# Fifty more unread TensorE products per image, in the filter's overhang and at the two ends of an image

## The chip, the core and the metric

The kernel runs on one core of a Trainium2 chip. The metric is the device time of one launch in microseconds (us), as the median of several runs. The core has five engines with their own instruction streams: TensorE (PE, matrix products; weight loads are shown as PEld), VectorE (DVE), ScalarE (ACT), GpSimd (POOL) and SyncE (SP, which issues the DMAs). They wait for one another by semaphores.

## The reference

The input is x, 16 images of 64 channels and 128 x 128 pixels. Two layers follow one another.

```python
# layer 0
q_in = jnp.quantile(x.reshape(B, C, -1), 0.5, axis=-1)      # a median per image and channel
x = x + relu(-q_in)[:, :, None, None]
y = upfirdn2d(x, lpf, up=2, padding=6, gain=4)              # 7 taps, along rows and columns
y = jnp.maximum(y, 0.0)
y = upfirdn2d(y, lpf, down=2)
# layer 1
spec = rfft2(x); mag = abs(spec)
gate = sigmoid(w2 @ gelu(w1 @ mag))
xf = x + irfft2(spec * gate)
q = xf @ q_w + q_b                                          # 16384 queries, 4 heads of 16
k, v = kv_path(8x8 convolution of xf), kv_path(16x16 convolution of xf)   # 256 + 64 keys
out = (softmax(q k / 4) v) @ proj_w + proj_b + x
```

## The kernel before

One loop runs over the 16 images, with a block for each engine in it. Each iteration does all of one image and, beside it, the median of the image after it. At its end every engine drains and meets the others at a barrier (L1416), SyncE clears the semaphores (L1422), a second barrier follows (L1423), and each engine jumps back to the start of the loop (L1415).

The stages of an image, as TensorE's program (`tensor`, from L392) has them:

1. The filter: 37 rounds n = 0 to 36 (P + 5, with P = 32 pairs of channels). In a round TensorE filters pair n along one direction (L463), pair n - 1 along the other (L473), takes pair n - 2 down again (L484), transposes pair n - 3 (L503) and takes two pairs that end with n - 4 down in the other direction (L494). Between these ScalarE (L1057, L1064) and VectorE (L834, L848, L841) copy the results out of PSUM. In the rounds 32 to 36, the overhang, no new pair enters and the last ones run out of the pipeline. `mid_up`, `mid_across` and `mid_down` (L432 to L450) compute a middle strip of the image every eighth round.
2. The forward transform: 17 rounds with L521 and L536 to L539; VectorE copies with L869 and L873.
3. Gate, inverse transform, convolutions, keys and values.
4. Attention over 32 groups of 512 queries, in 34 steps of ten parts; the last step of all ends with L763, L770 and VectorE's L1009.

The median search is a bisection in 26 steps. In a step VectorE (L304) and ScalarE (L247) each count values in three portions, TensorE adds the counts of two partitions (L203, L204), VectorE compares (L311 to L316), and the next step begins. It is written as generators (`pe_median`, `dve_median`, `act_median`, `pool_median`), which every engine's program advances at fixed places by `slot(n)`. So the order of the work on each engine is written out by hand. In a round of the filter the first `slot` stands behind L473 and, in the overhang, a second one at the round's end.

Unread products: `busy(bank, n)` issues n products of a constant with the identity, 128 x 128 by 128 x 512 in bfloat16, into a PSUM bank whose content nobody needs then. Nothing reads them and they signal nothing (L402). The kernel before has them at the start of an image (2), around the gate, between the small steps of the keys and values, in the first two groups of attention, and at the end of an image (2, 3 and 5 in the last step).

Of the kernel before, what the change touches and what calls it, by code (L numbers as in the profile page):

```python
# [29 lines left out]
P = C // 2  # L30
# [28 lines left out]
def program(nc, xa, xb, lev, msel, xh, small, sr1w, sr2w, out, nb=B):  # L59
    ctx = ExitStack()  # L60
    with ctx:
# [21 lines left out]
        def c(name, rows=128):  # L83
            o, w = SMALL[name]
            return cst[0:rows, o:o + w]
# [306 lines left out]
        def tensor(e):  # L392
# [3 lines left out]
            def slot(n):  # L396
                for _ in range(n):
                    next(med, None)

            def busy(bank, n):  # L400
                for _ in range(n):
                    e.matmul(ps[:, bank, :], lhsT=identb[:, :], rhs=cst[:, 0:256].bitcast(BF16), start=True, stop=True)  # L402

            busy(6, 2)

            def rest_up(b):
                e.wait_ge(xr, b + 1)
# [45 lines left out]
            for n in range(P + 5):  # L453
                if n < P and n % 8 < 3:
                    (rest_up, rest_across, rest_down)[n % 8](n // 8)
                if n < P:
                    if n:
                        e.wait_ge(t1, n)
                    for i in range(2):
                        x = XH[n // 4][:, 2 * (n % 4) + i, :]  # L460
                        for j in range(2):
                            r = slice(64 * j, 64 * j + 64)
                            op = e.matmul(ps[:, j, 133 * i:133 * i + 133], lhsT=x[r, :], rhs=ut[r, 133 * j:133 * j + 133],  # L463
                                          start=True, stop=True)
                    op.then_inc(up_ps, 1)
                m = n - 1
                if 0 <= m < P:
                    e.wait_ge(t1, m + 1)
                    if m:
                        e.wait_ge(yr, m)  # L470
                    for j in range(2):
                        r = slice(64 * j, 64 * j + 64)
                        op = e.matmul(ps[:, 2 + j, :].rearrange("p (c h n) -> p c h n", c=2, h=2),  # L473
                                      lhsT=ut[r, 133 * j:133 * j + 128],
                                      rhs=T1[m % 2][r].rearrange("p h c n -> p c h n")[:, :, :, 0:128], start=True, stop=True)
                    op.then_inc(yw_ps, 1)
                slot(1 if n > 1 else 0)
                m = n - 2
                if 0 <= m < P:
                    e.wait_ge(yr, m + 1)  # L480
                    if m:
                        e.wait_ge(vt, m)
                    for j in range(2):
                        op = e.matmul(ps[64 * j:64 * j + 64, 4, :], lhsT=c(f"d{j}"), rhs=Y[m % 2][:, j, :],  # L484
                                      start=True, stop=True)
                    op.then_inc(dn_ps, 1)
                m = n - 4
                if 0 <= m < P and m % 2:
                    gq = m // 2
                    e.wait_ge(vr, m + 1)  # L490
                    if gq:
                        e.wait_ge(zz, gq)
                    for j in range(2):
                        op = e.matmul(ps[64 * j:64 * j + 64, 6, :], lhsT=c(f"d{j}"), rhs=V[gq % 2][:, j, :, :],  # L494
                                      start=True, stop=True)
                    op.then_inc(z_ps, 1)
                m = n - 3
                if 0 <= m < P:
                    e.wait_ge(vt, m + 1)
                    if m:  # L500
                        e.wait_ge(vv, m)
                    for i in range(4):
                        op = e.transpose(ps[:, 5, 128 * i:128 * i + 128], VT[m % 2][:, 128 * i:128 * i + 128], c("ident"))  # L503
                    op.then_inc(tr_ps, 1)
                if n >= 8 and n % 8 < 3:
                    (mid_up, mid_across, mid_down)[n % 8](n // 8 - 1)
                slot(1 if n >= P or n % 4 == 0 and n > 8 else 0)

            for n in range(17):
                slot(1)  # L510
# [117 lines left out]
            def stage(g, j, bk):  # L628
                v0 = 16 * g + 4 * j
                bank = b7 if bk == 7 else b6  # L630
                e.wait_ge(*bank[0])
                if g == 0:
                    e.wait_ge(xfa, 8)
                e.matmul(ps[:, bk, :], lhsT=c("qw"), rhs=XFT[:, v0:v0 + 4, :], start=True, stop=True).then_inc(q_ps, 1)  # L634
                bank[0] = (qr, 4 * g + j + 1)
# [144 lines left out]
            for t in range(NT + 2):  # L780
                u, s4, ahead = t // 4, t % 4, t + AHEAD
                live, prev, done2 = t < NT, 0 <= t - 1 < NT, t >= 2
                for w in range(10):
# [17 lines left out]
                        denominators(t - 1)  # L801
                    if (t, w) in STAGES:
                        stage(*STAGES[t, w])
            busy(0, 5)

# [607 lines left out]
        with nc.Fori(0, nb, hint_back_edge=True) as it:  # L1415
            with nc.Block() as blk:  # L1416
                blk.sync(lambda e: sync(e, it))
                blk.gpsimd(gpsimd)
                blk.scalar(scalar)
                blk.vector(vector)  # L1420
                blk.tensor(tensor)
            nc.sync.sem_clear(cleared)  # L1422
            nc.all_engine_barrier()  # L1423
# [104 lines left out]
```

## Time and profile before

| | |
|---|---|
| median of 3 runs | 11891.15 us (11887.46 to 11897.37) |
| the profiled execution | 11873.21 us, its span 11871.9 us |
| PE busy | 10619.5 us (89%), 72913 matmuls |
| DVE busy | 8837.9 us (74%) |
| ACT busy | 7247.2 us (61%) |
| POOL busy | 2639.5 us (22%) |
| mean granted TensorE clock | 0.977 |

Busy is the share of the span in which an engine ran an instruction. The granted clock is the share of TensorE's full clock that the chip gave it, 1.00 for 2.4 GHz and 0.50 for 1.2 GHz; in a window it is the mean over the window. A clock under 1 in a window thus says for how much of it TensorE ran at half rate.

### The profile page before, as it was taken

Reading aid. Unit: us, or ns where it says so; the run is one execution under the profiler, and the core shown is the slowest. Engines: PE = TensorE matmul, PEld = TensorE weight load, DVE = VectorE, ACT = ScalarE, POOL = GpSimd, SP = SyncE. Lnnn points to the kernel's source line nnn. Section 1 sums busy time; section 2 is a strip of 40 time slices with the busy share of each in tenths; the row PEclk is TensorE's granted clock in tenths of the full one; section 3 lists DMA queues with packets and bytes.
Section 4 is the critical chain, followed back from the end, with each engine's and each line's share of the span. In section 5 each row is a group of like instructions: output and inputs, shape, how many; then the busy total and the mean of one; then the engine's idle time right before and its main releaser. Section 6 shows DMA issues by size and latency. Waiting matters only on the chain. (4 is left out here: it accounts for less than half of the span.)

```text
span 11871.9 us, 199727 instructions
## 1 busy us (share of the span) xinstructions
PE 10619.5 (89%) x72913; PEld 5396.2 (45%) x72913; DVE 8837.9 (74%) x15501; ACT 7247.2 (61%) x12109; POOL 2639.5 (22%) x4368
## 2 busy tenths in 40 slices
PE   1898998989989899898989989899898998989989
PEld 1544535344453544535435354453534445454453
DVE  6777777777777777777777777777777777777776
ACT  4656566665656656566565665656566565665656
POOL 1222313122131221312213121221312213122130
PEclk9999999999999999999999999999999999999999
DMA  2021120312212022130211202122021221202213
GB/s 56 27 43 48 42 66 20 53 38 48 60 30 57 23 53 56 33 62 24 50 51 40 65 23 45 46 44 64 24 53 34 50 59 30 57 23 54 55 34 74
DMA packets 176585, 537.89 MB, mean 45 GB/s; under 512 B 64873, under 2 KB 87401, under 8 KB 154033
## 3 DMA queue, kind: packets, MB, share of 16 engines
q1 hardware_dynamic: 175664, 525.24, 19.6%
q8 instruction: 624, 10.22, 0.4%
q14 instruction: 297, 2.42, 0.1%
HBM read 232.43 MB, written 71.30 MB: 26 GB/s over the span
## 5 line engine op out<-in xcount | busy, mean ns | idle before, releaser
L963 DVE TENSOR_REDUCE R<-ps 128x2 f32<-128x640 f32 x4096 | 3184.4, 818 | 880.3 <-PE ps L699 879.7
L1170 ACT ACTIVATE R<-ps 128x512 f32<-128x512 f32 x5120 | 2820.2, 594 | 638.7 <-PE ps L720 613.1
L247 ACT ACTIVATE R<-R,st 128x1475 bf16<-128x1475 f32 (+1 forms) x1326 | 2077.5, 1567 | 663.8 <-DVE st L316 639.0
L304 DVE TENSOR_SCALAR_CACHE_REDUCE R<-R,st 128x1255 bf16<-128x1255 f32 (+1 forms) x1326 | 1937.3, 1461 | 19.6
L699 PE MATMUL ps<-KST,R 96*128 96x320 bf16 x8192 | 1799.1, 300 | 35.7 <-DVE R L963 32.8
L745 PE MATMUL ps<-R 128*32 128x512 f32 x12288 | 1634.0, 604 | 37.9 <-DVE Wk L916 32.8
L720 PE MATMUL ps<-R,KST 104*128 104x512 bf16 x4096 | 1562.3, 384 | 37.6 <-ACT R L1170 28.0
L699 PEld LDWEIGHTS ps<-KST,R 96*128 96x128 bf16 x8192 | 753.9, 98 | 728.6 <-DVE R L963 218.6
L1253 POOL CAST R<-Wk 128x512 bf16<-128x512 f32 x256 | 283.8, 1109 | 2464.6 <-DVE Wk L916 2464.6
L720 PEld LDWEIGHTS ps<-R,KST 104*128 104x128 bf16 x4096 | 393.7, 97 | 718.6 <-ACT R L1170 467.6
L473 PE MATMUL ps<-R,cst 64*128 64x512 f32 x2048 | 570.3, 630 | 113.1 <-ACT R L1064 111.3
L370 POOL TENSOR_TENSOR R<-R,sB 128x1024 f32<-128x1024 f32 x136 | 255.7, 1897 | 1622.6 <-DMA R<-xh_in 1617.1
L1057 ACT ACTIVATE R<-ps 128x532 f32<-128x532 f32 x512 | 312.4, 610 | 489.5 <-PE ps L463 484.8
L1130 ACT ACTIVATE R<-ps,cst 128x512 bf16<-128x512 f32 x256 | 176.0, 688 | 691.0 <-PE ps L634 691.0
L484 PE MATMUL ps<-R,cst 128*64 128x512 f32 x2048 | 565.0, 631 | 21.1 <-ACT R L1064 21.1
L402 PE MATMUL ps<-cst,identb 128*128 128x512 bf16 x1776 | 512.9, 384 | 78.0 <-issue 54.1
L1177 ACT ACTIVATE Wk<-ps 128x256 f32<-128x256 f32 x512 | 196.7, 384 | 554.4 <-PE ps L763 554.4
L1064 ACT ACTIVATE R<-ps 128x1024 f32<-128x1024 f32 x512 | 517.7, 1011 | 21.7 <-PE ps L473 21.7
L1165 ACT ACTIVATE Wk<-ps 128x512 f32<-128x512 f32 x512 | 305.7, 597 | 368.9 <-PE ps L745 368.9
L203 PE MATMUL ps<-st,cst 128*128 128x6 f32 x884 | 168.2, 262 | 391.7 <-DVE R L304 159.8
L834 DVE COPY R<-ps 128x512 f32<-128x512 f32 x512 | 352.2, 688 | 156.1 <-PE ps L484 155.8
L1153 ACT ACTIVATE Wk<-ps 8x512 bf16<-8x512 bf16 x512 | 298.1, 582 | 268.9 <-PE ps L707 268.9
(208 smaller groups left out, 19297.2 us busy)
## 6 DMA issues: line engine op xcount, KB each, us to landing
R<-R SPq DMA_DIRECT2D x3072, 64.0 KB, 2.4
R<-xh_in SPq DMA_DIRECT2D x136, 512.0 KB, 4.4
out_dram<-Z SPq DMA_DIRECT2D x68, 1024.0 KB, 3.9
R<-xa_in SPq DMA_DIRECT2D x36, 1024.0 KB, 11.3
R<-xb_in SPq DMA_DIRECT2D x36, 1024.0 KB, 11.7
R<-sr_in SPq DMA_DIRECT2D x32, 1024.0 KB, 5.2
R<-sr_in SPq DMA_DIRECT2D x16, 2016.0 KB, 10.3
R<-sr_in SPq DMA_DIRECT2D x16, 1056.0 KB
```

Source lines behind the costliest of these rows:

```text
L247: e.activation(junka[:, 0:o2 - o1], xc[:, o1:o2], ACT.Sign, bias=mid, scale=-1.0, accum_out=cnt[:, NP + i:NP + i + 1]).then_inc(md_ca, 1)
L304: e.tensor_scalar(junk[:, 0:o1 - o0], xc[:, o0:o1], mid, None, ALU.is_le, ALU.add, accum_out=cnt[:, i:i + 1]).then_inc(md_cv, 1)
L402: e.matmul(ps[:, bank, :], lhsT=identb[:, :], rhs=cst[:, 0:256].bitcast(BF16), start=True, stop=True)
L473: op = e.matmul(ps[:, 2 + j, :].rearrange("p (c h n) -> p c h n", c=2, h=2), lhsT=ut[r, 133 * j:133 * j + 128], rhs=T1[m % 2][r].rearrange ...
L484: op = e.matmul(ps[64 * j:64 * j + 64, 4, :], lhsT=c(f"d{j}"), rhs=Y[m % 2][:, j, :], start=True, stop=True)
L699: op = e.matmul(ps[:, 2 + 2 * bq + r, 0:320], lhsT=q, rhs=KST[0:96, h0 + r, :], start=True, stop=True)
L720: op = e.matmul(ps[:, g2, :], lhsT=KST[:, h, c0:c0 + 128], rhs=QS[u % 3][:, h, 512 * s4:512 * s4 + 512], start=True, stop=True)
L745: op = e.matmul(ps[32 * h:32 * h + 32, 7, :], lhsT=VX[:, 4 * i + h, :], rhs=PB[:, k, src, :], start=i == 0, stop=i == 2)
L834: e.tensor_copy(VT[m % 2], ps[:, 4, :]).then_inc(vt, 1)
L963: e.tensor_reduce(MX[(4 * u + s4) % 2][:, blk_, h0:h0 + 2], ps[:, 2 + 2 * bq:4 + 2 * bq, 0:320], axis=AX.X, op=ALU.max).then_inc(mx, 1)
L1064: e.activation(Y[m % 2], ps[:, 2:4, :], ACT.Relu, scale=4.0).then_inc(yr, 1)
L1170: e.activation(PB[:, t % 2, w, :], ps[:, w % 2, :], ACT.Exp).then_inc(ex, 1)
```

## The change

It adds calls of `busy` in TensorE's program and changes three counts. At the start of an image there are 4 unread products instead of 2. In the rounds with n > P, which are n = 33, 34, 35 and 36, there are 5 behind the first `slot` and 6 behind the second, into bank 0. At the end of an image there are 9 instead of 5. That is 2 + 4 x 11 + 4 = 50 more per image. No other engine's program changes, and no wait is added or removed.

```diff
-            busy(6, 2)
+            busy(6, 4)
...
                 slot(1 if n > 1 else 0)
+                if n > P:
+                    busy(0, 5)
                 m = n - 2
...
                 slot(1 if n >= P or n % 4 == 0 and n > 8 else 0)
+                if n > P:
+                    busy(0, 6)
...
-            busy(0, 5)
+            busy(0, 9)
```

## Rows read from the trace of the kernel before

**Rows 1.** Page, costliest groups: busy, mean ns, idle before; clock of the core.

```profile
L402 PE MATMUL ps<-cst,identb 128*128 128x512 bf16 x1776 | 512.9, 384 | 78.0 <-issue 54.1
...
core 0: 11871.9 us, clock 0.977
```

**Rows 2.** L1198, GpSimd's clear at an image's start: all; from 1720; from 3885.

```profile
L1198 POOL MEMSET R<- x16: 1805/1805/1806, 272.6 to 11136.7; 128x2048 f32 x16
...
L1198 POOL MEMSET R<- x3: 1805/1805/1806, 1725.3 to 3165.6; 128x2048 f32 x3
...
L1198 POOL MEMSET R<- x2: 1805/1806/1806, 3890.0 to 4613.3; 128x2048 f32 x2
```

**Rows 3.** Windows behind an image's start: busy of PE, PEld, DVE, ACT, POOL; clock; DMA.

```profile
1725.00:1735.00 10.00, 8.00 (x54) 4.30 (x56) 3.35 (x4) 4.25 (x6) 3.00 (x7) 1.00 0.01 3
...
3890.00:3900.00 10.00, 7.85 (x34) 4.39 (x36) 0.65 (x2) 2.64 (x4) 2.19 (x4) 0.66 0.02 5
```

**Rows 4.** Windows over the filter's overhang in two images, same columns.

```profile
1151.00:1177.00 26.00, 13.33 (x69) 10.62 (x68) 22.38 (x47) 16.60 (x24) 7.40 (x14) 0.67 0.01 3
1874.00:1900.00 26.00, 13.15 (x57) 10.15 (x55) 21.00 (x44) 15.83 (x23) 6.68 (x12) 0.61 0.01 3
```

**Rows 5.** Timeline of PE at two boundaries: start, us, line, shapes, count, idle before.

```profile
994.78 1.24 PE L402 MATMUL ps<-cst,identb 128*128 128x512 bf16 x5
999.48 1.03 PE L402 MATMUL ps<-cst,identb 128*128 128x512 bf16 x2 [3.45 <-issue]
...
1726.88 0.60 PE L402 MATMUL ps<-cst,identb 128*128 128x512 bf16 x2 [3.12 <-issue]
```

**Rows 6.** The barrier at 996: ns min/median/max, first and last start.

```profile
L1416 PEldq DRAIN  x1: 1763/1763/1763, 994.3 to 994.3; - x1
L1416 DVEq DRAIN  x1: 458/458/458, 995.0 to 995.0; - x1
...
L1416 SPq DRAIN  x1: 7/7/7, 995.9 to 995.9; - x1
```

**Rows 7.** Timeline of PE in the overhang of the image at 997.

```profile
1148.89 1.08 PE L484 MATMUL ps<-R,cst 128*64 128x512 f32 x4 [1.32 <-ACT R L1064]
1149.80 1.03 PE L494 MATMUL ps<-R,cst 128*64 128x512 f32 x4
...
1154.18 0.36 PE L203 MATMUL ps<-st,cst 128*128 128x6 f32 x2 [2.27 <-DVE R L855]
...
1154.62 0.64 PE L503 MATMUL ps<-cst,R 128*128 128x128 f32 x4
...
1160.76 0.59 PE L203 MATMUL ps<-st,cst 128*128 128x6 f32 x2 [5.10 <-DVE R L304]
...
1161.70 1.98 PE L494 MATMUL ps<-R,cst 128*64 128x512 f32 x4
1167.70 0.59 PE L203 MATMUL ps<-st,cst 128*128 128x6 f32 x2 [4.02 <-DVE R L304]
...
1168.58 3.76 PE L521 MATMUL ps<-cst,Z 128*128 128x128 f32 x16
```

**Rows 8.** Timeline of DVE and POOL in the same stretch.

```profile
1158.59 0.68 DVE L848 COPY R<-ps 128x512 f32<-128x512 f32 x1
...
1163.96 0.68 DVE L841 COPY Z<-ps 128x512 f32<-128x512 f32 x1
...
1164.79 4.95 POOL L1230 TENSOR_TENSOR Z<-Z,R 128x512 f32<-128x512 f32 x4 [2.22 <-DVE Z L841]
...
1169.20 0.56 DVE L316 SCALAR_TENSOR_TENSOR st<-st 128x1 f32<-128x1 f32 x1
...
1172.88 0.69 DVE L869 COPY Wk<-ps 128x512 f32<-128x512 f32 x1
```

**Rows 9.** L869 in the images at 3890 and 6066.

```profile
L869 DVE COPY Wk<-ps x16: 678/684/687, 4062.9 to 4108.3; 128x512 f32<-128x512 f32 x16
...
L869 DVE COPY Wk<-ps x16: 678/686/687, 6241.7 to 6285.6; 128x512 f32<-128x512 f32 x16
```

## The prediction

> **What bounds the kernel now.** The page first: TensorE is the busiest engine, and 1776 of its instructions are unread products [rows 1]; over 16 images that is 111 for each. Its chain of waits ends in the last few per cent of the span and names no stage, so I went on by image. The mean granted clock is 0.977 of full [rows 1]: 2.3% of the span is missing, and as the lower level (1.2 GHz) is half of the upper (2.4 GHz), TensorE is at the lower one for 4.6% of the span, 546 us or 34 us per image. The clear at an image's start gives the period [rows 2]: (11136.7 - 272.6) / 15 = 724.3 us on average, but 720.15 us for the two images from 1725.3 on, and 723.3 us for the one at 3890.0. Windows of the same length show where this comes from: the ten microseconds behind an image's start have the clock at 1.00 in those two images (the first of them is shown) and at 0.66 in the other [rows 3]. There are 15 boundaries between images, and 13 show a clock under 1 (0.65 to 0.83). The overhang of the filter, on the other hand, loses the clock in every image: all 16 windows of 26 us there read 0.67 (eleven) or 0.61 (five), one of each in [rows 4]. These are the two places that the change touches, and what the unread products can win is the time that such a low stretch costs.
>
> The reader should see in the timelines why they occur. At the boundary TensorE ends its five unread products, sits idle 3.45 us and starts the next image with two [rows 5]. In the overhang it waits 5.10 us and 4.02 us for the counts of the median search, between short bursts [rows 7].
>
> **The end of an image: 4 products more.** Five products take 1.24 us, the last alone 0.38, so they follow each other every 0.215 us [rows 5]; four are 0.86 us. Are they hidden? TensorE's drain before the barrier starts at 994.3 and lasts 1.763, so it ends at 996.05; VectorE's starts at 995.0 and lasts 0.458, to 995.46, and SyncE's is at 995.9 [rows 6]. TensorE already comes last at the barrier, by about 0.2 us, and it is the unread products that make it last. So all of the 0.86 is paid, 16 times: 13.8 us. The barrier and the jump follow it, so the idle time of 3.45 us behind the products [rows 5] stays as long as it is.
>
> **The start: 2 more.** TensorE issues them before the first real product (L409), and ScalarE, VectorE and GpSimd wait for its first results, so nothing covers them. At full clock the pair lasts 0.60 us, at the low level 1.03 [rows 5]: 0.22 us or 0.43 us for each one. Two cost 0.43 to 0.86 us; I take 0.6, between the two because part of the boundaries already have the low level when they come and part lose it a little later. 16 x 0.6 = 9.6 us.
>
> **What these six may give back.** The low stretch at the boundary costs 723.3 - 720.15 = 3.15 us of an image [rows 2, 3]. The lower end of the gain is nothing, the upper is 13 of 15 boundaries saved: 13 x 3.15 = 41 us. The idle stretch is as long as before, and it is now preceded by 1.9 us instead of 1.1 us of such products. Two boundaries stay up today with the same products and a gap of 3.12 us before the restart instead of 3.45 [rows 5], so the outcome hangs on little; but as the cause, the gap, isn't touched, I put the value near the lower end: one boundary in ten, 5 us.
>
> The Trainium skill ("TensorE: Matmul & The Clock Gate", in the section on HAM oscillation) says that it is the wait between two bursts that brings the clock down, every time it comes, and that a kernel gets out of it by laying its products out without that wait. By that rule the 5 us would be 0, and it speaks against this part of the change. The clock of 0.66 behind the 3.45 us gap agrees, the two boundaries at 1.00 don't quite.
>
> **The overhang: 11 more in each of four rounds** (n = 33 to 36; n = 32 is left out by n > P). Together with the six this is 50 per image. Round by round, at full clock:
> - n = 33, first five: TensorE is idle 1.32 us before L484 for ScalarE's L1064 [rows 7]. 5 x 0.215 = 1.08 us fit in: nothing.
> - n = 33's six and n = 34's five lie between the pair product L203 at 1154.18 and the transposes L503 at 1154.62 [rows 7]. L503 comes 11 x 0.215 = 2.4 us later and ends at about 1157.6. VectorE reads it in L848, which started only at 1158.59 because two counts of 1.5 us stood before it [rows 8]. Hidden, with 0.9 us to spare. At the low level the eleven take 4.7 us, L503 ends near 1160, and L848, the third count and the next pair product behind it come 0.7 to 1.3 us later.
> - n = 35's five stand before L494, between the pair product at 1160.76 and VectorE's L841 at 1163.96. L494 lasts 1.98 us at the low level and 1.03 at the upper [rows 7], so five products (1.08 us) and a quick L494 end when the slow one did: nothing. At the low level: 2.15 us late.
> - n = 36's eleven and the six behind the product at 1167.70 end before or about when L521 is wanted; L521 takes 3.76 us at the low level for 16 instructions [rows 7], and VectorE takes its first result only at 1172.88, behind its own counts [rows 8]: nothing.
>
> What does a full clock give there? The pair product L203 with L204 is on the path of the median search, which sets the pace of these rounds: L203 lasts 0.36 at the upper level and 0.59 at the lower [rows 7], with L204 likewise some 0.4 us per trip. There are two slow trips. The second is partly hidden: L316 behind it takes 0.56 us at 1169.20, beside GpSimd's L1230, which runs from 1164.79 for 4.95 us [rows 8]. So 0.4 to 0.8 us per image. Against it: TensorE still waits 2.27 us before L203 at 1154.18 [rows 7], and no product is put there, so in perhaps half of the images the clock still falls and the eleven products meet it low, at 0.7 to 1.3 us. The two nearly cancel: I take a gain of 0.2 us, 16 x 0.2 = 3 us (bounds: +16 x 1.3 = 21 us lost, -16 x 0.8 = 13 us won).
>
> A further gain lies behind the overhang. In images whose low stretch is the long one (clock 0.61), the 16 copies L869 of the first transform go from 4062.9 to 4108.3, 45.4 us; in the image at 6066 they take 43.9 us [rows 9]. The long form of the stretch reaches into these rounds, where TensorE is the bound, and costs 1.5 us. Unread products right up to L521 end it sooner. Five of 16 images: 7.5 us.
>
> **The sum.** 13.8 + 9.6 - 5 - 3 - 7.5 = +7.9 us on the profiled execution, whose time is 11873.2 us (span 11871.9): 11881. That execution lies 18 us below the median of the runs, 11891.15; moved onto it the forecast is 11899 us, 0.07% above.
>
> **The rivals.**
> - B, faster: the clock stays up at the boundary. For it: images at 1725 and 2445 did just that with two products, and they kept it for two images running, as their period nearly repeats; nine dense products may be enough. Then 41 us are won, the start's two cost 0.43 instead of 0.6 (6.9 us), and the sum is 13.8 + 6.9 - 41 - 3 - 7.5 = -31 us: 11860. Against it: the gap of 3.45 us is untouched.
> - C, slower: the unread products run at the low level. The place is n = 34 and 35 of the overhang; the price is L503 and L494 late by 1.3 us net in every image, no gain behind the overhang, and 0.86 + 0.86 us at the boundary with nothing back: (1.3 - 0.4 + 1.72) x 16 = 42 us, 11933. It decides if the clock still falls behind the 2.27 us wait in most images. For it: that wait has no cover.
> - D, the change doesn't do what it says: the clock does the same as today in both places, and in the overhang the extra products find only slack. What is left is the boundary, 13.8 + 16 x 0.86 = 27.6 us: 11919, close to the bound between no change and slower.
>
> **How the numbers follow.** My own forecast 43%, B 27%, C 20%, D 10%. About 0.2% (24 us) is what a measurement of this kernel tells from no change, so faster means under 11867 and slower over 11915. B is faster, with 2 points of the forecast's own tail: 29%. C and half of D are slower: 25%. The rest, 46%, is the same. The forecast's own range is 11875 to 11915. For 8 in 10 I reach down to 11850, past B's centre, and up to 11932, to C's centre.
>
> **What would show it.** In the changed profile 2576 unread products instead of 1776. TensorE's drain before the barrier 0.86 us longer behind VectorE's. The windows of 26 us at the overhang well above 0.67, near 0.9, or else C. The number of boundaries with a clock under 1: about 12 of 15 for me, few for B. L848 behind the eleven products: at once behind its count for me, waiting for TensorE in C. The span of the 16 L869 copies never at 45.4 by a long low stretch. I am wrong if the period of an image in which nothing falls isn't about 721 us, or if most boundaries keep the clock.

## The result, and the profile after

The changed kernel took 11851.6 us (six runs, 11842.6 to 11859.5) against 11891.4 us (six runs). The ratio is 0.9964, with a 95% interval of 0.9954 to 0.9974: 0.36% faster, where 0.07% slower was forecast. The time lies 2 us inside the lower end of the 8-in-10 range (11850 to 11932 us) and outside the forecast's own range (11875 to 11915 us); the direction was wrong. A second measurement of the same kernel (e9 below) gave 11832.3 us, ratio 0.9942 (0.9926 to 0.9959). The two differ by 19 us, more than any term of the prediction's sum, and the runs don't show why. The change alters two counts (2 to 4, 5 to 9) and adds two calls of `busy`.

The page of the kernel after, part 1; its weight loads are 73713 instead of 72913, which are the 50 x 16 added products. Of the unread products the trace has 2400 product records and 2576 weight loads; some product records are missing, and the 2576 are the number that was forecast. Then the mean clock, and the clear at an image's start, L1202 now:

```profile
PE 10723.2 (90%) x73537; PEld 5423.0 (46%) x73713; DVE 8880.7 (75%) x15501; ACT 7248.1 (61%) x12109; POOL 2633.7 (22%) x4368
...
core 0: 11858.2 us, clock 0.989
...
L1202 POOL MEMSET R<- x16: 1804/1806/1807, 272.5 to 11124.1; 128x2048 f32 x16
```

The period of an image is (11124.1 - 272.5) / 15 = 723.4 us, 0.8 less than in [rows 2]. The windows of ten microseconds behind an image's start, as in [rows 3]; three of 15, and all 15 show a clock of 1.00, where 13 of 15 had less:

```profile
996.00:1006.00 10.00, 9.14 (x61) 4.67 (x64) 4.63 (x5) 5.00 (x8) 3.26 (x8) 1.00 0.08 29
3888.00:3898.00 10.00, 9.49 (x61) 4.74 (x64) 4.70 (x5) 5.07 (x8) 3.02 (x7) 1.00 0.10 36
11124.00:11134.00 10.00, 9.56 (x61) 4.74 (x64) 4.84 (x5) 5.21 (x8) 3.06 (x8) 1.00 0.11 42
```

Why the clock stays up is in TensorE's timeline at the first boundary, the counterpart of [rows 5], and in the drains before the barrier, the counterpart of [rows 6]:

```profile
992.90 2.11 PE L402 MATMUL ps<-cst,identb 128*128 128x512 bf16 x9
996.74 0.81 PE L402 MATMUL ps<-cst,identb 128*128 128x512 bf16 x3 [1.74 <-PEq L1427]
```

```profile
L1420 PEldq DRAIN  x1: 2622/2622/2622, 992.4 to 992.4; - x1
L1420 DVEq DRAIN  x1: 460/460/460, 993.1 to 993.1; - x1
L1420 SPq DRAIN  x1: 7/7/7, 994.0 to 994.0; - x1
```

TensorE's drain is 2.622 us instead of 1.763: the 0.86 us of the four products is paid at the barrier, as forecast. But the idle time behind it is 1.74 us instead of 3.45 (1.7 to 1.8 at all 15 boundaries, where it was 3.1 to 3.9). The barrier isn't shorter: in both kernels TensorE's jump back to the loop's start begins just under 1 us behind the end of its drain. The jump itself is shorter. It has a row of its own in TensorE's queue, min/median/max of the 16 in ns (the smallest is the last one, which doesn't jump back): first the kernel before, then after.

```profile
L1415 PEldq COMPARE_BRANCH  x16: 88/2519/2789, 997.0 to 11859.6; - x16
```

```profile
L1419 PEldq COMPARE_BRANCH  x16: 87/358/404, 996.0 to 11846.8; - x16
```

2.5 us became 0.36. The DMA view shows what differs at the jump. Queue q8 brings code: 624 packets and 10.22 MB on the page of either kernel, 16384 bytes each. Between 984 and 996 us the kernel before has no packet on q8, and one comes at the jump (window 996 to 999; it lies at 996.6, 0.4 us before the jump begins). The kernel after has that packet in the window 984 to 995, at 984.6, some 11 us before its jump, and none from 995 to 996.4 around it. In both one more packet follows, some 0.7 us behind the jump's end. Before, then after (packets, MB, share of 16 engines in the window):

```profile
q8 instruction: 1, 0.02, 2.7%
```

```profile
q8 instruction: 1, 0.02, 1.0%
```

The overhang, as in [rows 4], in the images at 996 and 3888, and TensorE's timeline in the first of them, as in [rows 7]:

```profile
1149.00:1175.00 26.00, 22.80 (x117) 16.00 (x116) 23.54 (x47) 19.16 (x30) 9.28 (x16) 0.89 0.01 3
4041.00:4067.00 26.00, 21.50 (x113) 13.81 (x115) 22.55 (x46) 18.20 (x26) 8.55 (x17) 0.93 0.01 3
```

```profile
1146.69 3.62 PE L402 MATMUL ps<-cst,identb 128*128 128x512 bf16 x11
1150.11 1.06 PE L505 MATMUL ps<-cst,R 128*128 128x128 f32 x4
...
1153.48 0.36 PE L203 MATMUL ps<-st,cst 128*128 128x6 f32 x2 [0.62 <-DVE R L304]
...
1160.48 0.39 PE L203 MATMUL ps<-st,cst 128*128 128x6 f32 x2 [1.83 <-DVE R L304]
...
1160.95 2.07 PE L402 MATMUL ps<-cst,identb 128*128 128x512 bf16 x6
1162.82 3.02 PE L525 MATMUL ps<-cst,Z 128*128 128x128 f32 x16
```

The clock is 0.89 and 0.93 there, and 0.87 to 1.00 over the 16 images, as forecast, and L203 takes 0.36 us at the two trips that took 0.59. But the first eleven products take 3.62 us, where eleven at full clock take 2.5 (the second eleven of each image do): the clock falls for a while under them, and L505 (L503 before) takes 1.06 us instead of 0.64 behind them. This happens in 11 of the 16 images (3.6 to 4.2 us), where the prediction had it in half.

### The profile page after: what moved, and what is told of

It is laid out like the page before. It is cut to its first block and busy times, and to the rows that moved or that the text cites. A ratio compares the mean times of both kernels' runs of the same rounds, so it can differ in the third digit from the quotient of the medians.

```text
span 11858.2 us, 201151 instructions
## 1 busy us (share of the span) xinstructions
PE 10723.2 (90%) x73537; PEld 5423.0 (46%) x73713; DVE 8880.7 (75%) x15501; ACT 7248.1 (61%) x12109; POOL 2633.7 (22%) x4368
## 3 DMA queue, kind: packets, MB, share of 16 engines
q8 instruction: 624, 10.22, 0.4%
## 5 line engine op out<-in xcount | busy, mean ns | idle before, releaser
L402 PE MATMUL ps<-cst,identb 128*128 128x512 bf16 x2400 | 676.3, 392 | 62.3 <-PEq L1427 25.8
L749 PEld LDWEIGHTS ps<-R 128*32 128x32 f32 x12288 | 247.5, 108 | 457.0 <-issue 365.8
```

The lines of the kernel that those rows point to most:

```text
L749: op = e.matmul(ps[32 * h:32 * h + 32, 7, :], lhsT=VX[:, 4 * i + h, :], rhs=PB[:, k, src, :], start=i == 0, stop=i == 2)
```

## The experiments

A block of code is taken here as what one packet brings, 256 instructions in 16384 bytes; e15 below tests this. **Theory F** (fetch of code): the jump is quick when the loop's end lies far enough behind the start of its block, and the added products moved it there by adding 100 instructions to the loop (a weight load and a product each). **Theory C** (clock): the products themselves keep the clock up or give the jump time. The first pair takes them apart: the place without products, and the products without the place. e1 moves the loop's start too, which the change doesn't; but with the start where it was the jump is slow before and quick after the change, so it is the place of the end that is tested.

```diff
  # e1: the kernel before, 100 instructions more ahead of the loop, run once
  # (two waits make one instruction)
   e.wait_ge(vm, 1)
+  for _ in range(200):
+      e.wait_ge(in_c, 16)
   for _ in pe_median(e, Bank7()):
```

> The kernel before, with 200 more waits on a semaphore that is already set, in TensorE's part ahead of the loop (100 more instructions of its code, run once while it waits anyway). Nothing in the loop changes, only where the loop lies in TensorE's code: its end is 100 instructions further on, as in the changed kernel. Theory F (code fetch): the gain is TensorE's jump back to the loop's start, which takes 2.0 to 2.8 us in the kernel before and 0.36 us in the changed one, because the last block of code is entered earlier. Then this kernel has a jump of about 0.4 us, an idle gap of about 1.3 us at the boundary, no boundary with a clock under 1, and is faster than before by 33 us for the jumps and up to 41 us for the clock: 11815 to 11855 us. Theory C (clock): the unread products keep the clock up, and the jump is short because they are there. Then the jump stays at 2.0 to 2.8 us and the time at 11891 us.

```diff
  # e2: the changed kernel, 156 instructions more ahead of the loop
+  for _ in range(312):
+      e.wait_ge(in_c, 16)
```

> The changed kernel with all its 50 unread products, and 312 such waits ahead of the loop (156 instructions), so that the end of the loop lies where it does in the kernel before, counted in blocks of 256 instructions. Theory F: the jump takes 2 to 2.8 us again, the idle gap at the boundary is about 3.5 us, most boundaries show a clock under 1, and the time is what the prediction's own sum gave, 11880 to 11915 us. Theory C: the jump stays at 0.36 us and the time at 11850 us.

```diff
  # e3: only the overhang, 2 and 5 products at the ends
-  busy(6, 4)
+  busy(6, 2)
...
-  busy(0, 9)
+  busy(0, 5)
```

> Only the 44 products in rounds 33 to 36; 2 at the start and 5 at the end as before. The loop's code is 88 instructions longer. Theory F: the jump is 0.4 us, no clock under 1 at the boundaries, and without the 0.86 us at the end and 0.43 us at the start it is faster than the changed kernel by 16 x 1.3 = 21 us: 11830 us. Theory C: the boundaries lose the clock as before (13 of 15), the jump is 2 us or more, 11880 to 11895 us.

```diff
  # e4: the kernel before with
-  busy(6, 2)
+  busy(6, 4)
...
-  busy(0, 5)
+  busy(0, 9)
```

> Only the products at the two ends, 4 and 9; none in the overhang. The loop's code is 12 instructions longer. Theory F: the last block of code is entered 12 instructions earlier, which is about 1 to 2 us earlier because the drain and the barrier lie between, so the jump is shortened in part, to 0.4 to 2 us, and the time lies between 11850 and 11900 us. Theory C: the boundaries keep the clock by the products at them, and the time is 11850 to 11870 us with a jump of 0.36 us.

Measured, with ratios to the kernel before in the same call (11893.1 us): e1 11822.6 us, 0.9940 (0.9923 to 0.9957). e2 11895.5 us, 0.9999 (0.9989 to 1.0008). e3 11823.5 us, 0.9936 (0.9920 to 0.9953). e4 11865.4 us, 0.9981 (0.9970 to 0.9992). A clock under 1 shows at none of the 15 boundaries of e1 and e3, at 13 of e2 and at 7 of e4. The jump in e1, e2 and e4:

```profile
L1417 PEldq COMPARE_BRANCH  x16: 88/358/426, 994.1 to 11807.2; - x16
```

```profile
L1421 PEldq COMPARE_BRANCH  x16: 87/3020/4120, 992.6 to 11877.6; - x16
```

```profile
L1415 PEldq COMPARE_BRANCH  x16: 88/1767/1929, 997.1 to 11845.5; - x16
```

This decides for F. Nothing in the loop of e1 differs from the kernel before, and it gains at least what the changed kernel does (0.9940, against 0.9964 and 0.9942); all 50 products of the change are in e2, and nothing is left of the gain. e4 shows a part that belongs to C: the jump is shortened to 1.8 us, by about the 0.86 us that the four products at the end take. But e2 has the same nine products at the end and a jump of 3.0 us in the median, between 1.3 and 4.1, so it isn't quite the jump of the kernel before, and the products don't shorten the jump at every place.

The next call asks what the gap, the ends' products and a small shift are worth.

```diff
  # e5: e1, with 4 and 9 products at the ends
  # e6: e1, with a wait for GpSimd's clear at an image's start
+  e.wait_ge(zcl, 1)
   busy(6, 2)
  # e7: e1, without the products at the ends
-  busy(6, 2)
...
-  busy(0, 5)
  # e8: the kernel before, 24 waits (12 instructions) ahead of the loop
```

> The shifted kernel (200 waits ahead of the loop, quick jump) with the 4 and 9 products at the two ends, none in the overhang. The prediction's own terms say what these six products cost when nothing comes back for them: 0.86 us at the end and 0.43 us at the start at full clock, 16 x 1.29 = 21 us: 11843 us, against 11822.6 us for the shifted kernel. The rival says that they also spare a clock loss somewhere behind the boundary, then it is 11825 us or less.

> The shifted kernel, where TensorE waits at the start of each image for GpSimd's clear (L1198 of the kernel before), which ends 1.8 us behind the start of its image. This puts an idle gap of 3 to 3.3 us back at the boundary, by a wait and not by the jump; the jump itself stays at 0.4 us. If it is the gap that brings the clock down, most boundaries show a clock under 1 again and the time is within 10 us of the kernel before, 11880 to 11895 us. If the slow jump costs the clock in another way (or the clock at the boundary is worth little), the boundaries stay at 1.00 and only the wait is paid: 16 x 1.5 = 24 us over 11822.6, 11847 us.

> The shifted kernel with no unread product at the start and none at the end of an image (the loop is 14 instructions shorter, its end 86 further on than in the kernel before). With a quick jump the gap is short without them. What they cost goes: 0.43 us at the start and the 0.2 us by which TensorE comes last at the barrier, 16 x 0.6 = 10 us: 11812 us. The rival: the gap is now 1.1 us longer in front and the work behind it sparse, so the clock falls again at part of the boundaries, 2 to 3 us each: 11825 to 11850 us.

> The kernel before with 24 waits ahead of the loop (12 instructions), so that the loop's end lies where it does with the products at the two ends alone, but without those products. Theory F (the place of the loop's end in the code sets the jump): the jump takes 1.3 to 1.9 us as there, the gap is about 2.9 us, half of the boundaries keep the clock, and the time is 11850 us, some 15 to 20 us under that run because the products' own cost is not paid. Theory C (the products shortened the jump by giving it time): 2.0 to 2.8 us for the jump and 11885 us.

Measured beside 11893.9 us for the kernel before: e5 11825.0 us, 0.9940 (0.9924 to 0.9957). e6 11876.7 us, 0.9986 (0.9976 to 0.9995). e7 11829.0 us, 0.9947 (0.9929 to 0.9965). e8 11907.0 us, 1.0010 (0.9999 to 1.0020). e6's boundary, its jump still at 0.358 us; TensorE's timeline and two of its windows:

```profile
996.30 1.24 PE L402 MATMUL ps<-cst,identb 128*128 128x512 bf16 x5
1001.15 0.38 PE L402 MATMUL ps<-cst,identb 128*128 128x512 bf16 x1 [3.60 <-POOL R L1199]
```

```profile
999.00:1009.00 10.00, 7.85 (x43) 4.35 (x46) 2.46 (x3) 3.54 (x6) 2.78 (x6) 0.83 0.01 3
2449.00:2459.00 10.00, 8.77 (x53) 4.80 (x56) 3.40 (x4) 4.27 (x6) 1.64 (x5) 0.83 0.00 0
```

So it is the gap that costs the clock, and the slow jump isn't needed for it: 3.6 us by a wait bring the low level back at all 15 boundaries, and 54 us with it over e1, of which the wait itself is 16 x (3.6 - 1.75) = 30 us. The other 24 us, 1.6 us per boundary, are left for the clock. The expectation was 3 us too high at the least. The length of the gap isn't all: in e4 the clock stayed up behind two gaps of 3.24 us and fell behind one of 2.79 us. e5 came out at 11825 us, at the rival's value, where my term of 21 us was expected; but four runs lay between 11817 and 11841, so it can't be told from half of that term. e7 gained nothing, as its rival said: its gap is 2.5 us, 5 of 15 boundaries lose the clock, and 11829 us doesn't beat e1. e8 was a miss: 12 instructions leave the jump at 2.7 us (its row is below) and all 15 boundaries lose the clock, so in e4 it wasn't the place that shortened the jump, it was the products.

The third call has the changed kernel again with its terms taken singly, and a larger shift.

```diff
  # e9: the changed kernel, nothing else
  # e10: the changed kernel with
-  busy(0, 9)
+  busy(0, 5)
  # e11: the changed kernel with
-  busy(6, 4)
+  busy(6, 2)
  # e12: the kernel before, 80 waits (40 instructions) ahead of the loop
```

> The changed kernel once more, unchanged, on the chip of its two variants. 11850 us if its place against the other kernels is its own; near 11825 us if the difference to the overhang's or the ends' products alone was one of chips or of chance.

> The changed kernel with 5 products at the end of an image instead of 9 (4 at the start, 44 in the overhang); its loop's end lies 92 instructions further on than in the kernel before, so the jump stays quick. By the prediction's term (TensorE comes last at the barrier and pays each product) it gains 13.8 us: 11837 us. If the 28 us between the changed kernel and the overhang alone lie in the clock's windows elsewhere and not in this term, it is anywhere between 11820 and 11850 us, and its shortest image is still 0.86 us shorter than that of the changed kernel.

> The changed kernel with 2 products at the start instead of 4 (9 at the end, 44 in the overhang). By the prediction's term at full clock it gains 16 x 0.43 = 7 us: 11844 us; the same alternative as for the variant with 5 at the end.

> The kernel before with 80 waits ahead of the loop (40 instructions). With 12 the jump stayed slow, with 100 it was quick. TensorE enters the last block of its code some microseconds earlier, in the last step of the attention. If the fetch of the loop's start begins when that block is entered and takes about 3 us until the code can run, 40 instructions put it 3 to 5 us ahead of the jump: jump 0.4 to 1 us, time 11820 to 11850 us. If it begins later than the entry by some 40 instructions' worth, the jump stays at 2 us or more and the time at 11890 us.

Measured beside 11893.7 us: e9 11832.3 us, e10 11822.0 us, 0.9933 (0.9916 to 0.9949), e11 11834.8 us, 0.9948 (0.9929 to 0.9966), e12 11919.5 us, 1.0020 (1.0009 to 1.0031). e9 lies nearer to the 11825 us of chance or of the chip than to 11850. e10 is 10 us under it, where the term of the four end products was 13.8, and e11 2 us over it; the intervals, some 20 us to either side, are wider than the terms, so neither is resolved. The other sign named for e10 failed: its shortest image isn't 0.86 us shorter than that of the changed kernel, it is 720.1 us against 719.9, and 719.7 in e9. e12 missed again: the jump stays at 2.6 us, all 15 boundaries lose the clock, and the time is 0.2% above the kernel before, for which neither way had a reason. So I ran three more shifts, each one execution with its profile: 64, 176 and 256 instructions (128, 352 and 512 waits, same place).

> The kernel before with 64 more instructions of TensorE's code ahead of the loop. 40 left the jump slow, 88 and 100 made it quick. If the fetch that counts is moved from behind the barrier to one wait of the last attention step earlier, there is a step between 40 and 88 and no slope: the jump is either 0.4 us or 2 us and more. If it is a slope, it is about 1 us.

> The same with 176 instructions. If it is enough that the last block is entered long before the jump, the jump stays at 0.4 us and the fetch before it comes more than 11 us ahead of it; 11820 us.

> The same with 256 instructions, a whole block. If the place within a block of 256 instructions (16384 bytes, the size of one fetch) is what counts, the loop's end is where it is in the kernel before: the jump takes 2.0 to 2.8 us and the time is 11890 us. If the waits ahead of the loop, or the loop's absolute place, had another effect, the jump is 0.4 us and the time 11820 us.

One run each, beside a single 11910.6 us for the kernel before: 11840.4, 11831.5 and 11882.0 us. Times of single runs say little here (18 runs of the kernel before in one call lay between 11861 and 11922 us); the jumps are read from 15 boundaries each. The jump with 12, 40, 64 and 256 instructions (e8, e12, e13, e15), one row each:

```profile
L1417 PEldq COMPARE_BRANCH  x16: 87/2702/3109, 995.2 to 11897.7; - x16
```

```profile
L1417 PEldq COMPARE_BRANCH  x16: 87/2589/2769, 999.6 to 11907.6; - x16
```

```profile
L1417 PEldq COMPARE_BRANCH  x16: 88/444/506, 1003.7 to 11827.8; - x16
```

```profile
L1417 PEldq COMPARE_BRANCH  x16: 88/2779/2914, 995.9 to 11868.3; - x16
```

Medians in us by the shift of the loop's end: 2.52 (0), 2.70 (12), 2.59 (40), 0.44 (64), 0.40 (86, e7), 0.36 (88, e3), 0.36 (100), 0.36 (176, e14), 2.78 (256), and 3.02 for e2, which is 256 as well, 100 in the loop and 156 ahead of it. It is a step between 40 and 64, and it repeats with 256 instructions, the content of one 16384-byte packet.

The times of the q8 packets, found with narrow windows of the DMA view, show what the jump waits for. First the kernel before (window 996.5 to 996.7), then e13 (window 1001.1 to 1001.2), each with its first jump:

```profile
q8 instruction: 1, 0.02, 41.0%
...
L1415 PEldq COMPARE_BRANCH  x1: 2345/2345/2345, 997.0 to 997.0; - x1
```

```profile
q8 instruction: 1, 0.02, 28.2%
...
L1417 PEldq COMPARE_BRANCH  x1: 506/506/506, 1003.7 to 1003.7; - x1
```

At all 90 boundaries of the kernel before, e2, e4, e8, e12 and e15 the jump ends 2.3 to 3.1 us behind this packet, whether the packet comes 1.6 us ahead of the jump's start or 1.6 us behind it. In e13 it comes 2.5 to 4.3 us ahead, in e1 and e3 about 10, in e14 about 17 (more than 11 was expected), and the jump takes 0.51 us at the most. So the jump waits for this code. The four more products of e4 begin the jump later (the packet is 0.7 to 1.6 us ahead of it, against 0.8 at the most in the kernel before), which is why it is shorter. Why the packet comes when it does, and so why the step lies between 40 and 64, is open; that it follows TensorE's entry into the last block is argued only, and e2 and e15, at the same place, have it at different times.

The Trainium skill ("Runtime: NRT & Kernel Launch", section "Instruction fetch mechanics") states that code is brought in blocks of 16 KiB, 256 instructions, one ahead of the one in execution, and that a jump to a block that isn't there has to wait for its fetch. The packets of 16384 bytes, the jump of 2.5 us and the repetition at 256 agree.

## Why the prediction was wrong

**The step that failed** is in the part on the end of an image: "The barrier and the jump follow it, so the idle time of 3.45 us behind the products [rows 5] stays as long as it is." It became 1.74 us. I took the jump's time as a property of the chip and didn't open its row, which showed 2.0 to 2.8 us on TensorE alone in each of 15 boundaries. The change's 100 instructions moved the loop's end by 100 in its block of 256, and e1 shows that this alone is worth 0.60% (0.43 to 0.77), 70 us: 15 jumps x 2.16 us = 32 us, and 38 us that are left for the clock behind them, for which 41 us stood in rival B. The 38 us are a remainder and not measured alone; e6 leaves 24 us for the clock at 15 boundaries, so its worth isn't settled. Most boundaries kept the clock, which the prediction had named as a sign of being wrong. B was right on what happens (no boundary falls) and wrong on the cause: not "nine dense products", since e1 keeps the clock with five and two.

**The sum without that step** came out in total. e2 is the changed kernel with the old place; its ratio is 0.9999 (0.9989 to 1.0008), and 1.0007 was forecast. In part this is luck: its jump is half a microsecond longer than that of the kernel before, and the terms below don't each come out. Term by term:

- The end's 0.86 us: the drain grew from 1.763 to 2.622 us, as forecast. In e4, with a late packet, 0.75 us of it come back in the jump (1.77 us instead of 2.52). With a quick jump nothing in the trace gives it back, but the times don't resolve it (e10 against e9: 10 us, 13.8 forecast; the shortest images: nothing). What the sum left out is that whether the end is paid depends on the jump behind it.
- The start's 0.6 us: at full clock now (3 recorded products in 0.81 us), so 0.43; in times it isn't resolved (e11).
- "One boundary in ten": all 13 were saved, by the shorter gap. The forecast's reason, that the gap is the cause, is what e6 shows. At the old place e2 loses 13 of 15 with the added products (12 forecast).
- The overhang's net 3 us and the transform's 7.5 us: e3 against e1 is 11823.5 to 11822.6 us, nothing that intervals of some 20 us to either side can show. The traces have both halves. From first to last start the 32 copies of L848 (L852) take 144.6 us in e1 and 145.2 in e3, on average over 16 images: the clock falls under the first eleven in 14 images of e3, L503 comes late, and VectorE waits 0.5 us for it (17 waits, 9.3 us), as in rival C, at half its price. The 16 copies of L869 (L873) take 45.5 and 44.7 us. The two about cancel. The prediction's reading of these copies was wrong: they take 45.3 us or more in 15 of 16 images of the kernel before, whether the overhang's clock is 0.61 or 0.67, so 45.4 isn't the mark of the long low stretch, and "five of 16 images" has no basis. Its sign, that they are never at 45.4, fails as well: 7 of the changed kernel's 16 images are there or above, with the long low stretch gone. One image of each as an example, at 2435 in e1 and at 2443 in e3:

```profile
L848 DVE COPY R<-ps x32: 673/680/685, 2446.0 to 2590.5; 128x512 f32<-128x512 f32 x32
...
L869 DVE COPY Wk<-ps x16: 677/684/687, 2604.8 to 2650.3; 128x512 f32<-128x512 f32 x16
```

```profile
L852 DVE COPY R<-ps x32: 676/680/692, 2454.1 to 2599.2; 128x512 f32<-128x512 f32 x32
...
L873 DVE COPY Wk<-ps x16: 677/684/687, 2613.6 to 2657.4; 128x512 f32<-128x512 f32 x16
```

- The clock in the overhang near 0.9: 0.87 to 1.00. A higher clock there is worth no time that can be seen: the mean clock of the whole is 0.989 in the changed kernel's profile and 0.980 in that of e1, which is no slower.

None of the 50 products is needed for the gain: e1 without them, 11822.6 us, and e10 with 46 of them, 11822.0 us, can't be told apart, and both beat the kernel as changed in its first measurement.

## What to carry to other kernels

A change that adds instructions to a loop also moves the loop's end in the code. Before pricing what the instructions do, look at the jump's row and at the code packets around it: if one engine's jump takes microseconds and the others' don't, try some tens to a hundred and more instructions ahead of the loop (here 12 and 40 did nothing, 64 did), which run once and cost nothing that shows here, and measure any variant at more than one place. A gain of unread products is theirs only if it stays when the place is put back.

## What the runs showed of the hardware

- TensorE's jump at the loop's end takes 0.36 to 0.51 us or 1.9 to 3.1 us with the same loop (the kernel before, e1, e8, e12 to e15), by the place of its end within 256 instructions; the slow ones end 2.4 to 3.0 us behind a code packet. The other engines' jumps at the first boundary of the kernel before took under 0.1 us, the longest of them VectorE's:

```profile
L1415 DVEq COMPARE_BRANCH  x1: 90/90/90, 996.9 to 996.9; - x1
```

- A gap of 1.5 to 1.8 us between images left the clock at 1.00 in every boundary (the changed kernel, e1, e3, e5, e9 to e11, e13, e14); with 2.5 us 5 of 15 lost it (e7), with 2.6 to 3.3 us 7 (e4), with 3.6 to 3.8 us by a wait all 15 (e6). A higher mean clock doesn't mean a shorter time: e2's profile has 0.989 where the kernel before has 0.977, and their times are the same.
